# Message records of 129 numbers, chunks that begin at any row, and 560 gather tiles in a three-layer graph kernel

## The reference

```python
x = emb[x_ids]                                  # 12500 x 128
for W_a, b_a, W_b, b_b in layers:               # three layers
    msg = vals[:, None] * x[col]                # 400000 edges x 128
    h = segment_sum(msg, row, num_segments=N)   # N = 12500
    z = (h + x) @ W_a.T + b_a + h * x @ W_b.T + b_b
    x = where(z >= 0, z, 0.2 * z)
```

## Time and profile before

| | |
|---|---|
| median of 3 runs | 9024.51 us (9022.02 to 9027.93) |
| the profiled execution | 9031.06 us |
| its span | 9029.1 us |
| mean granted TensorE clock | 0.953 |
| moved by DMA | 1720.76 MB, 191 GB/s in the mean |

### The profile page before, as it was taken

How to read it: one execution, slowest core, us unless ns; L and a number is a source line. 1 busy time by engine, 2 the same in 40 slices (tenths; PEclk the granted TensorE clock), 3 DMA queues, 4 the chain that set the end, 5 groups by cost and what they waited for, 6 DMA issues and landing times.

```text
span 9029.1 us, 250958 instructions
## 1 busy us (share of the span) xinstructions
PE 8034.0 (89%) x80584; PEld 7367.7 (82%) x80585; DVE 7105.5 (79%) x10046; ACT 4550.7 (50%) x14200; POOL 5617.2 (62%) x3637
## 2 busy tenths in 40 slices
PE   7699997899996588899999788799999788899999
PEld 4577775677775488899999788799999788899999
DVE  7699997899996877677777777777777777777777
ACT  0699993499996266621111566611112566511112
POOL 8677772388785133378887233388886233488884
PEclk8799998899998699999999999999999899999999
DMA  2211111011115988888888588888887688888886
GB/s 84 39 7 7 7 7 18 10 7 7 7 7 29 95 307 310 306 285 283 286 287 279 174 306 310 303 283 287 287 286 237 219 306 310 298 285 286 287 286 200
DMA packets 1005648, 1720.76 MB, mean 191 GB/s; under 512 B 378356, under 2 KB 429624, under 8 KB 1004920
## 3 DMA queue, kind: packets, MB, share of 16 engines
q0 software_dynamic: 378656, 958.17, 35.5%
q1 hardware_dynamic: 499680, 753.27, 23.5%
q10 hardware_dynamic: 127224, 8.24, 3.7%
HBM read 963.06 MB, written 756.12 MB: 190 GB/s over the span
## 4 chain that ended last, share of the span: by engine, by line
PE 59%; ACT 19%; issue 10%; DVE 5%; POOL 3%; DMA 2%; ACTq 1%; DVEq 1%; SPq 0%; POOLq 0%
PE ps L969 36%; PE ps L960 18%; ACT hT L670 17%; POOL xb L495 2%; DVE work L1323 2%; PE ps L804 2%; DMA messages<-work 2%; DVE hT L1286 1%; PE ps L997 1%; PE ps L977 1%; PE ps L998 1%; ACT run_idx L657 1%; DVE work L1336 1%; ACT work L728 0%; ACT stage L659 0%
## 5 line engine op out<-in xcount | busy, mean ns | idle before, releaser
L969 PE MATMUL ps<-work 128*128 128x125 f32 x28416 | 3282.2, 278 | 46.7 <-DVE work L1352 31.5
L969 PEld LDWEIGHTS ps<-work 128*128 128x128 f32 x28416 | 3240.5, 192 | 88.5 <-DVE work L1352 33.1
L562 POOL DMA_INDIRECT work<-messages,work x1776 | 2705.7, 1523 | 620.6 <-issue 609.0
L960 PE MATMUL ps<-xb,work 125*128 x10752 | 1919.5, 223 | 445.9 <-DVE work L1323 432.1
L1352 DVE TENSOR_TENSOR work<-work,iota_p 128x1000 f32<-128x1000 f32 x1776 | 2119.2, 1193 | 1.0 <-issue 0.6
L547 POOL PARTITION_BROADCAST work<-work x672 | 892.2, 1328 | 1858.7 <-DMA work<-slot_cols 928.5
L728 ACT ACTIVATE work<-ps,work 128x128 f32<-128x128 f32 x5376 | 1532.4, 368 | 970.5 <-PE ps L960 933.4
L960 PE MATMUL ps<-hT,work 125*128 x10752 | 1913.6, 222 | 0.0
L960 PE MATMUL ps<-work 125*128 x10752 | 1907.7, 221 | 0.0
L746 ACT ACTIVATE work<-work 128x8 f32<-128x8 f32 x1776 | 534.4, 301 | 2676.2 <-DMA work<-messages,work 2672.8
L854 PEld LDWEIGHTS ps<-hT 128*128 128x128 f32 x12768 | 1485.4, 196 | 313.2 <-ACT stage L659 182.7
(11 more groups left out here) (212 smaller groups left out, 5842.8 us busy)
## 6 DMA issues: line engine op xcount, KB each, us to landing
messages<-work SPq DMA_DIRECT2D x2688, 256.0 KB, 3.3
work<-messages,work POOLq DMA_INDIRECT x1776
out_x<-xb SPq DMA_DIRECT2D x150, 125.0 KB
sorted_edges<-stage,run_idx POOLq DMA_INDIRECT x798
work<-slot_cols SPq DMA_DIRECT2D x672, 4.0 KB
work<-lane_places SPq DMA_DIRECT2D x532, 5.2 KB
out_x<-xb ACTq DMA_DIRECT2D x4, 1562.5 KB
sorted_edges<-hT SPq DMA_DIRECT2D x4, 908.0 KB
```

The costliest lines, as they stand in the source:

```text
L562: pool.indirect_dma_start(out=ck[:, n, :, :].rearrange("p h x -> p (h x)"), out_offset=None, in_=flat, in_offset=bass.IndirectOffsetOnAxis ...
L960: last = t.matmul(ps[:, n % PR, j * D:(j + 1) * D], col_hot[:, at:at + P], piece[:, bass.ds(offs[n], D)], start=k == 0, stop=k == 2)
L969: last = t.matmul(part[n], ck[:, n, j // CH, j % CH * D:(j % CH + 1) * D], sel[:, n % SELB, j, :], start=j == 0, stop=j == CHB - 1)
```

## The change

A message record is now that of one edge: 128 values and its row number, 129 numbers; four of them take the same 516 numbers as the old record. A lane of a tile reads eight records in a row from any edge on, so fewer lanes and tiles are needed: TB is 560. The row numbers no longer lie in the DRAM tensor ahead of time. They are turned by TensorE and kept by ScalarE before the layers (`row_of`, 16-bit integers), and in every layer GpSimd copies those of two groups into two message buffers (`put_rows`), once the last stores of both have landed; SyncE waits for it before it stores, and stores all 516 numbers per lane. In GpSimd's program the spread of the next batch stands ahead of the two copies of a batch, and each spread waits for the copies before it and for its own end. SyncE asks for a column row six batches ahead of the store it stands at, instead of four, and waits before it for the spread of two batches on. The DMA of ScalarE goes. Shifted positions of the tables follow.

```diff
-TB = -(-((E + (2 * (CH - 1) + CH) * NB * NB) // CHB // P + 1 + NB) // (2 * BU)) * 2 * BU
+ROWF = D + 1
+TB = -(-((E + (CHB - 1) * NB * NB) // CHB // P + 1 + NB) // (2 * BU)) * 2 * BU
...
-        messages = dram("messages", [CHUNKS + CHB // CH, CH * D + CH])
+        messages = dram("messages", [SLOTS2 + CHB, ROWF])
...
-        msg = work[:, MSG0:MSG0 + MR * GE].rearrange("p (n x) -> p n x", n=MR)
+        REC = CH * ROWF
+        msg = work[:, MSG0:MSG0 + MR * REC].rearrange("p (n j e) -> p n j e", n=MR, j=CH)
...
-                def spread_cols(i, first):
+                def put_rows(i, n, first):
+                    for k in (n, n + 1):
+                        if k >= MR:
+                            pool.wait_ge(msg_stored[k % MR], la * (GROUPS // MR * DMA) + i * (AU // MR * DMA) + (k // MR) * DMA)
+                        elif not first:
+                            pool.wait_ge(msg_stored[k % MR], la * (GROUPS // MR * DMA) + i * (AU // MR * DMA))
+                    taken_up()
+                    g.tensor_copy(msg[:, n % MR:n % MR + 2, :, D],
+                                  row_of[:, bass.ds(i * (AU * CH) + n * CH, 2 * CH)].rearrange("p (n j) -> p n j", j=CH)).then_inc(rows_put, 1)
+
+                def spread_cols(i, h, first):
+                    pool.wait_ge(col_src_in[h], la * (ABODIES * DMA) + i * DMA + DMA)
+                    if not first or h >= CR2:
+                        pool.wait_ge(col_hot_ready, la * (GROUPS // 2) + i * (AU // 2) + (h + 1 - CR2) * BATCH // 2)
+                    if not first or h >= 2:
+                        pool.wait_ge(rows_put, la * (GROUPS // 2) + i * (AU // 2) + (h - 1) * (BATCH // 2))
+                    taken_up()
+                    g.partition_broadcast(col_row[:, h % CR2, :], col_src[h * 32:h * 32 + 1, :], channels=P).then_inc(col_spread[h], 1)
+                    pool.wait_ge(col_spread[h], la * ABODIES + i + 1)
+
+                def spread_body(i, first, last):
                     for h in range(CB):
...
+                        if h + 1 < CB:
+                            spread_cols(i, h + 1, first)
+                        elif not last:
+                            spread_cols(i + 1, 0, False)
+                        for n in range(h * BATCH, (h + 1) * BATCH, 2):
+                            put_rows(i, n, first)
...
-                def store_messages(i, last):
+                def store_messages(i, left):
                     for n in range(AU):
-                        if n % BATCH == 0 and not last:
-                            sp.wait_ge(col_spread[n // BATCH], la * ABODIES + i + 1)
-                            load_cols(i + 1, n // BATCH)
+                        h = n // BATCH
+                        if n % BATCH == 0 and h < CR2 and left >= 1:
+                            sp.wait_ge(col_spread[CR2 + h], la * ABODIES + i + 1)
+                            load_cols(i + 1, CR2 + h)
+                        if n % BATCH == 0 and h >= CR2 and left >= 2:
+                            sp.wait_ge(col_spread[h - CR2], la * ABODIES + i + 2)
+                            load_cols(i + 2, h - CR2)
+                        if n % 2 == 0:
+                            sp.wait_ge(rows_put, la * (GROUPS // 2) + i * (AU // 2) + (n // 2 + 1))
+                            sp.sem_inc(stores_begun, 1)
                         sp.wait_ge(msg_ready[n % 2], la * (GROUPS // 2) + i * (AU // 2) + (ACREDIT + n // 2 + 1))
-                        sp.dma_start(messages[bass.ds(i * (AU * P) + n * P, P), 0:CH * D], msg[:, n % MR, :]).then_inc(msg_stored[n % MR], DMA)
+                        sp.dma_start(records[bass.ds(i * (AU * P) + n * P, P), :], msg[:, n % MR, :, :].rearrange("p j e -> p (j e)")).then_inc(msg_stored[n % MR], DMA)
...
-            act.dma_start(messages[0:CHUNKS, CH * D:REC].rearrange("(p c) j -> p c j", p=DP), slot_row).then_inc(slots_stored, DMA)
...
+            for k in range(GPP):
+                act.wait_ge(rows_turned, k + 1)
+                s.activation(row_of.rearrange("p (t k j) -> p k j t", k=GPP, j=CH)[:, k, :, :],
+                             ps[:, k, 0:CH * DP].rearrange("p (j t) -> p j t", j=CH), ACT.Copy).then_inc(rows_kept, 1)
...
-                            last = t.matmul(part[n], ck[:, n, j // CH, j % CH * D:(j % CH + 1) * D], sel[:, n % SELB, j, :],
+                            last = t.matmul(part[n], ck[:, n, j, 0:D], sel[:, n % SELB, j, :],
...
-            link(v.tensor_tensor(m[2], m[1], m[0], ALU.add))
-            rounded(m[3], m[1], -(CH - 1) / 2, 1.0 / CH)
-            rounded(m[4], m[2], (CH - 1) / 2, 1.0 / CH)
-            link(v.tensor_tensor(m[5], m[4], m[3], ALU.subtract))
-            rounded(m[5], m[5], (HALVES - 1) / 2, 1.0 / HALVES)
-            link(v.tensor_scalar(m[0], m[0], 0.5, None, ALU.is_ge))
-            link(v.tensor_tensor(m[6], m[5], m[0], ALU.mult))
+            rounded(m[6], m[0], (CHB - 1) / 2, 1.0 / CHB)
```

More of the change, by code:

```diff
@@ L21 @@
 I32 = mybir.dt.int32
+I16 = mybir.dt.int16
 U8 = mybir.dt.uint8
@@ L85 @@
 BU = 8
-TB = -(-((E + (2 * (CH - 1) + CH) * NB * NB) // CHB // P + 1 + NB) // (2 * BU)) * 2 * BU
-assert CHB == 2 * CH and (E + NB * (CH + GE - 1)) // GE <= GROUPS
+ROWF = D + 1
+TB = -(-((E + (CHB - 1) * NB * NB) // CHB // P + 1 + NB) // (2 * BU)) * 2 * BU
+assert (E + NB * (CHB - 1 + GE - 1)) // GE <= GROUPS
 BBODIES = TB // BU
@@ L98 @@
 assert HTW >= N
-assert HSORT <= HTW and TB == 592 and GROUPS % AU == 0 and AU == CB * BATCH and AU % MR == 0
+assert HSORT <= HTW and TB == 560 and GROUPS % AU == 0 and AU == CB * BATCH and AU % MR == 0
 UNITS = [P, GE]
@@ L113 @@
 ROUND = 12582912.0
-WORKW = 22032
+WORKW = 23760
 def graph_layers(nc, ids, row, col, vals, emb, weights, biases, out):
@@ L552, in _ @@
+                with pool.Fori(1, ABODIES - 1) as i:
+                    spread_body(i, False, False)
+                spread_body(ABODIES - 1, False, True)
                 for n in range(MR):
                     pool.wait_ge(msg_stored[n], la * (GROUPS // MR * DMA) + GROUPS // MR * DMA)
-                pool.wait_ge(slots_stored, DMA)
                 taken_up()
@@ L584, in _ @@
                     sp.dma_start(to[:, k * size:(k + 1) * size], zeros[:, 0:size]).then_inc(zero_filled, DMA)
-            sp.dma_start(messages[CHUNKS:CHUNKS + HALVES, :], zeros[0:HALVES, 0:REC]).then_inc(zero_filled, DMA)
+            sp.dma_start(messages[SLOTS2:SLOTS2 + CHB, :], zeros[0:CHB, 0:ROWF]).then_inc(zero_filled, DMA)
             def load_rows(p, i, q, first):
@@ L913, in _ @@
                 last.then_inc(vals_turned, 1)
+            pe.wait_ge(rows_found, 1)
+            for k in range(GPP):
+                pe.wait_ge(vals_kept, k + 1)
+                for j in range(CH):
+                    last = t.transpose(ps[:, k, j * DP:(j + 1) * DP],
+                                       slot_row[:, k * GE:(k + 1) * GE].rearrange("p (m j) -> p j m", j=CH)[:, j, :], ident[:, :])
+                last.then_inc(rows_turned, 1)
             when_asked()
@@ L1040, in _ @@
             link(v.tensor_scalar(not_dummy[:, :], iota_c[:, :], float(NB), None, ALU.is_lt))
-            for k, at in enumerate((DUMPS[0], DUMPS[1], CHUNKS)):
+            for k, at in enumerate((DUMPS[0], DUMPS[1], SLOTS2)):
                 v.tensor_scalar(dummy_at[:, k:k + 1], not_dummy[:, :], -float(at), float(at), ALU.mult, ALU.add)
@@ L1220, in _ @@
             rounded(number, rec, -(P - 1) / 2, 1.0 / P)
-            v.tensor_scalar(slot_row, number.rearrange("p (c j) -> p c j", j=CH), -1.0, None, ALU.add).then_inc(rows_found, 1)
+            v.tensor_scalar(slot_row, number, -1.0, None, ALU.add).then_inc(rows_found, 1)
             for g in range(GPP):
@@ L1278, in _ @@
             link(v.tensor_copy(split(tt[3]), ps[0:NBD, 4:6, 0:TB // 2]))
-            for k, part_ in enumerate((4096.0, 64.0)):
+            for k, part_ in enumerate((16384.0, 128.0)):
                 rounded(tt[4], tt[3], 0.0, 1.0 / part_)
@@ L1305, in _ @@
                     v.tensor_tensor(rest[:, at], x_flat[:, at], x_high[:, at], ALU.subtract).then_inc(rest_ready, 1)
-                dve.wait_ge(slots_stored, DMA)
+                dve.wait_ge(rows_kept, GPP)
                 for c in range(SPLITS):
```

66 lines of the change are left out of this document (34 added, 32 removed).

## The result

The changed kernel takes 9122.99 us in the median of four runs (9116.28 to 9127.8), the kernel before beside it 9023.26 us (9020.63 to 9027.93): ratio **1.0111 [1.0098, 1.0123]**, slower. The forecast was 9084 us, slower, with a range from 8900 to 9220.

A forecast was written before the change was run, and what follows sets the result against it. TensorE bounds the kernel before; after the change a ring of waits binds the message stage. 9031.1 - 177.4 (tiles) - 8.5 (tables) + 245 (ring) = 9090, with the median 6.6 lower: 9084 us, range 8900 to 9220.

The forecast's parts named there:

- The ring over eight groups through SyncE's wait: Message stage: landing, copy, spread, SyncE's wait and four stores form a loop of 7.55 us per eight groups, +245 us.
- the step to the broadcast: Message stage, GpSimd: from a copy's end to the next spread's start, 0.20 us of the eight-group loop.
- Tiles: Sum stage: 592 to 560 tiles at 1.848 us each on TensorE, three layers, -177.4 us.
- Gathers from odd rows: Sum stage, a rival: gathers 25% dearer become the bound, 9270 us with the ring; chance 0.03.
- Tables: Before the layers: fewer table turns, fewer linked instructions, narrower tables, -8.5 us; added transposes and copies are covered.
- The VectorE slowdown: Message stage: GpSimd's eight short copies add at most some 2.4 us per body to VectorE, hidden.
- ScalarE's DMA of row numbers: Before the layers: its removal from a queue with nothing behind it was costed at nothing.
- the sum of 9090: Whole kernel: profiled 9031.1 us with tiles, tables and ring added, before taking off 6.6 us for the median.
- The earlier request alone is worth nothing: Message stage: asking for column rows twelve groups ahead saves no time by itself.
- The ring does not bind: Message stage, a rival: the body stays at 13.64 us and only savings are left, 8838 us; chance 0.14.
- Stores become dearer: Message stage, a rival: new source start addresses make stores cost more, +67 us, 9151 us; chance 0.13.
- The clock: Message stage, a rival: TensorE's clock falls, at half speed +1900 us, some 10700 us; chance 0.02.

The follow-up runs named there:

- e1: Changed kernel with SyncE asking five batches ahead, so waiting for the next batch's spread: 8804.54 us, 0.9746 of the kernel before.
- e6: Changed kernel with GpSimd spreading two batches ahead of its copies, SyncE left as it was: 8813.59 us, 0.9767 of the kernel before.
- e8: Changed kernel with SyncE's wait and column load moved behind the batch's four stores, still six batches ahead: 8798.44 us, 0.9746 of the kernel before.
- e12: e1 with ScalarE's DMA of 114688 pieces put back, to a tensor that nothing reads: 8817.49 us, 0.9769 of the kernel before.
- e7: Changed kernel with SyncE asking four batches ahead, as the kernel before did: 8806.23 us, 0.9754 of the kernel before.
- e4: Changed kernel with ScalarE and VectorE writing row numbers, no GpSimd copies and no SyncE waits for them: 8824.73 us, 0.9774 of the kernel before.
- e3: Kernel before with 560 tiles in place of 592 and nothing else: 8844.13 us, 0.9795 of the kernel before.
- e11: Same kernel as e5, run on another chip beside e9 and e10: 9097.53 us, 1.0076 of the kernel before.
- e5: Changed kernel with ScalarE's DMA of 114688 pieces put back, to a tensor that nothing reads: 9074.31 us, 1.0053 of the kernel before.
- e9: Changed kernel unaltered, run again beside e10 and e11 on one chip: 9085.0 us, 1.0059 of the kernel before.
- e10: e5 with the added tensor kept but only 128 pieces written: 9087.83 us, 1.0065 of the kernel before.
- e2: Changed kernel with every GpSimd copy of row numbers made twice, the second after the first's end: 9210.67 us, 1.02 of the kernel before.

## Why the prediction was right, and where it was not

- **The ring over eight groups through SyncE's wait** was the mechanism. e1, e6 and e8 each cut it at another place, and each brings the message stage to 753 to 765 us. Cover for the waits was rightly denied: every step was found in the trace with 0.05 us or less between forecast and median.
- **Its length was mis-sized**, by some 0.2 us in 7.55, and 168 bodies of two turns make +63 us of that (+308 against +245). The copy took 0.20 us and not 0.15, the landing was seen after 0.23; rounding 7.58 down gave away another 0.03. The rest lies between the sum of medians (7.61) and the mean period (7.75), by the means above: the terms were read as typical cases, and a ring is paid by the mean. The largest part is the step to the broadcast, forecast at 0.20 from one event and 0.28 in the mean. The copies beyond 0.20 us add 0.02; they are those beside a one-hot of VectorE (220 of 626 such copies took over 0.3 us, of the other 718 all but 4 took 0.20).
- **Tiles**: -178.9 us with the dense stages, -177.4 forecast. Gathers from odd rows took 1527 ns in the mean of the whole span, before 1523. Right, and that rival is out.
- **Tables**: -8.9 us of -8.5, right, including the cover of transposes and copies. The VectorE slowdown stayed hidden; indeed the one-hots (now L1367) fell from 650 to 485 ns. Before, a broadcast overlapped 580 of the 1344, which took 881 ns in the mean where the others took 474; in the changed kernel it overlaps 42.
- **The step that failed**: "ScalarE's DMA of row numbers disappears from a queue with nothing behind it: nothing". Nothing was behind it in its queue, but the transfers of SyncE's queue landed late beside it. Without it the tables came 22.2 us sooner by the two chains, and putting it back cost 17.7 us in e12. This error and the ring's had opposite signs: 63.4 - 27.9 - 1.5 = 34 us, the distance of the profiled 9124 from the sum of 9090. That the forecast came so near is in part luck.
- **The earlier request alone is worth nothing**: right, by e7 against e1.
- **"The ring does not bind"** is out by the waits. **"Stores become dearer"** found nothing for it: the profile of the changed kernel has a DMA share of 0.75 for 273 GB/s, before 0.85 for 307, the same share for each GB/s to 1%, and e4 and e3 agree to 1% too. The fourth store landed after 3.10 us, as the sum had it without that price. Landings don't speak for it: e1's stores have the new start addresses and land after 3.1 us in the median, e3's have the old and land after 3.1 on the same chip (e4's, also new, take 3.6, which stays unexplained, with no loss of time; so a price on landings alone isn't ruled out). The rule of the Trainium skill, "DMA: Bandwidth & Descriptors", "How a descriptor splits into AXI transactions", would have them 6% dearer by the prediction's estimate (68 beats for 64); the rows of e4 and e3 don't show it.
- **The clock** stayed at 0.97 in the message stage, with TensorE idle a fifth of it.

What stays open: why e1 and e8 have message stages up to 10 us shorter than before (VectorE's one-hots go with it: 504 to 512 ns in e1, e7, e8 and e12 with stages of 753 to 762 us, 654 to 682 ns in e3, e4 and e6 with 760 to 765, but no run set them apart); what in a body makes the step to the broadcast 0.46 us in one batch of four; why e4's stores land later; and what about the places makes the landing differ.

## What to carry to other kernels

Where a request is moved ahead, write down everything that is queued behind its new wait, and follow that until it comes back to the releaser: if it does, the sum of the steps over the groups it spans, landings included, is a floor under the time, whatever the engines' busy shares. The cure may be only to put the wait behind the work it held up (e8) or to look one step less far ahead (e1). Sum a ring from means over many turns and not from single events. And cost a transfer of many small pieces by what it does to the transfers beside it, even when its own queue is otherwise empty.

## What the runs showed of the hardware

- One DMA of 114688 pieces of 16 B took 158 to 182 us, and beside it a transfer of 2.5 KB landed after 9.4 to 11.7 us (e11, e5, e12, before); without it the same transfer took 1.8 to 1.9 (the changed kernel, e1, e9, e10).
- The landing of a 258 KB store went with the spacing of the stores, but not with that alone: on chip 0 the median was 3.1 us in e1 at 13.5 us per body, 3.6 in e4 at 13.6 and 2.7 in e2 at 15.9. In the changed kernel the four of a batch, issued within 1.75 us, landed after 2.6, 2.9, 3.1 and 3.1 us.
- The same ring-bound kernel had 0.14 us more or less in its landings from one place to another, and with it 38 us in its time (9122.99 and 9085.0), where the kernel before, without a ring, moved by 4. The four runs in one place spread over 12 and 15 us.
- VectorE's one-hot of 125x1024 took 474 ns in the mean with no broadcast of GpSimd beside it and 881 with one (before). A copy of 128x8 numbers by GpSimd took 0.20 us, and over 0.3 in 220 of the 626 cases with a one-hot beside it (the changed kernel).
